# A fused eight-batch transformer kernel: front of the cross stage in halves, shared one-hots, final sums on TensorE

## The reference, cut to what matters

```python
ln1 = _layer_norm(hidden_states, ln1_weight, ln1_bias)      # cross stage begins
qkv = jnp.einsum('sbh,oh->sbo', ln1, qkv_weight)
... # causal attention, projection
h1 = hidden_states + proj
ln2 = _layer_norm(h1, ln2_weight, ln2_bias)
logits = x @ router_weight                                   # x is ln2 by token
top_p, top_i = jax.lax.top_k(probs, K)                       # K = 2
...
dst = jnp.where(valid, sorted_exp * cap + within, T)
padded_tokens = jnp.zeros((T, H), x.dtype).at[dst].set(x[order // K], mode='drop')
fc1 = jax.nn.gelu(jnp.einsum('ech,ehf->ecf', xt, moe_w1))
fc2 = jnp.einsum('ecf,efh->ech', fc1, moe_w2).reshape(T, H)
moe_out = jnp.zeros((N, H)).at[padded_tid].add(fc2 * padded_probs[:, None])
return h1 + moe_out.reshape(S, B, H)     # then x = x + gb * (this), the layer's gate
```

## Time and profile before

| | us |
|---|---|
| median of the runs | 3152.18 |
| the profiled execution, own time | 3159.02 |
| its span | 3157.3 |
| cross stage, from its first to its last instruction | 2499.9 to 2754.5 |
| routing, to the last instruction of the table of slots | 2754.8 to 2802.9 |
| experts, first gather to last copy | 2803.8 to 3108.5 |
| last scatters, final sums, stores | 3108.5 to 3157.3 |

### The profile page before, as it was taken

One profiled execution on the slowest core, in us unless ns is written; L12 is line 12 of the kernel. 1 busy time (PEld: TensorE's weight loads), 2 busy tenths in 40 slices (PEclk: granted clock), 3 DMA queues, 4 the chain that ended last, 5 costly groups with the idle time before them and its releaser, 6 DMA issues. The chain is left out here.

```text
span 3157.3 us, 53117 instructions
## 1 busy us (share of the span) xinstructions
PE 2904.5 (92%) x20820; PEld 1968.8 (62%) x20820; DVE 1646.8 (52%) x5006; ACT 1403.8 (44%) x3081; POOL 836.2 (26%) x831
## 2 busy tenths in 40 slices
PE   6889999878999999999999999999999688899993
PEld 3566666654666757576666666665656444478883
DVE  4667776645555544544444444445554488631114
ACT  3666666632535444444444444534444124132222
POOL 1001111113333332332323222233333311025551
PEclk8999999999999999999999999999999899789997
DMA  4111111004000000000010000000000000112325
GB/s 139 18 19 20 18 20 20 8 3 164 8 4 10 6 16 30 1 1 1 13 33 1 1 1 5 28 14 11 6 6 11 11 1 27 53 41 79 73 83 186
DMA packets 66232, 93.95 MB, mean 30 GB/s; under 512 B 9971, under 2 KB 52982, under 8 KB 64944
## 3 DMA queue, kind: packets, MB, share of 16 engines
q1 hardware_dynamic: 58304, 74.24, 8.0%
q0 software_dynamic: 7680, 16.32, 2.0%
HBM read 59.31 MB, written 27.36 MB: 27 GB/s over the span
## 5 line engine op out<-in xcount | busy, mean ns | idle before, releaser
L1343 PE MATMUL bank<-h2T,w 128*128 128x512 f32 x1024 | 478.9, 606 | 5.3 <-ACT gT L1281 3.7
L1381 PE MATMUL bank<-w,gT 128*128 128x256 f32 x2048 | 465.9, 381 | 0.0
L1381 PEld LDWEIGHTS bank<-w,gT 128*128 128x128 f32 x2048 | 379.3, 190 | 49.7 <-issue 0.5
L1018 POOL TENSOR_TENSOR prob<-prob,rsum 128x512 f32<-128x512 f32 (+1 forms) x256 | 237.7, 949 | 591.0 <-DVE rsum L1165 591.0
L1343 PEld LDWEIGHTS bank<-h2T,w 128*128 128x128 f32 x1024 | 182.2, 190 | 224.0 <-issue 173.7
L1281 ACT ACTIVATE gT<-bank,vec 128x512 f32<-128x512 f32 x256 | 175.1, 687 | 285.6 <-PE bank L1343 284.2
L583 ACT ACTIVATE y<-y,least 128x128 f32<-128x128 f32 (+3 forms) x512 | 252.2, 555 | 52.4 <-DVE least L463 52.3
L463 DVE CUSTOM_DVE_ANT_0 y<-bank,mask 128x128 f32<-128x128 f32 (+3 forms) x512 | 223.9, 486 | 71.9 <-PE bank L680 71.0
L1171 DVE COPY probT<-bank 128x1024 f32<-128x1024 f32 (+1 forms) x128 | 139.3, 1088 | 226.7 <-PE bank L1397 226.7
L1142 DVE CUSTOM_DVE_ANT_0 prob<-bank,mask 128x256 f32<-128x256 f32 (+1 forms) x512 | 164.3, 386 | 168.1 <-PE bank L1333 168.1
L1253 ACT ACTIVATE prob<-prob,least 128x256 f32<-128x256 f32 (+1 forms) x512 | 239.9, 473 | 15.8 <-DVE least L1142 15.5
(11 more groups left out here) (313 smaller groups left out, 5010.7 us busy)
## 6 DMA issues: line engine op xcount, KB each, us to landing
w<-in_W SPq DMA_DIRECT2D x8, 1024.0 KB, 5.9
expert_parts<-zeros SPq DMA_DIRECT2D x8, 1024.0 KB, 16.2
we<-in_we SPq DMA_DIRECT2D x16, 512.0 KB
rows<-modulation SPq DMA_DIRECT2D x40, 128.0 KB, 2.9
x<-in_x SPq DMA_DIRECT2D x8, 512.0 KB, 6.3
prob<-score SPq DMA_DIRECT2D x64, 64.0 KB, 2.4
probT<-score SPq DMA_DIRECT2D x64, 64.0 KB, 2.4
token_rows<-rows_normed SPq DMA_DIRECT2D x4, 1024.0 KB, 4.4
```

Of the source, the lines that this page charges most:

```text
L1018: nc.gpsimd.tensor_tensor(two, two, rsum[:, at:at + 2].unsqueeze(2).to_broadcast([P, 2, width]), ALU.mult).then_inc(s["probs"], 1)
L1343: ins = nc.tensor.matmul(M[m % 2][:, :], w1[:, k, m * P:(m + 1) * P], h2T[:, k, :], start=(k == 0), stop=(k == KD - 1))
L1381: ins = nc.tensor.matmul(M[i][:, (t % 2) * D:(t % 2 + 1) * D], gT[:, m, t * P:(t + 1) * P], w2[:, m, :], start=(m == 0), stop=(m == MF - 1))
```

## The change

It has four parts. **(a)** The front of group 0 goes in two halves of four tiles with semaphores of their own (`front_stats`, `front_rstd`, `front_norm`); the clearing of banks 4 and 5 moves behind it and behind the statistics of group 1; PE runs 6 `idle_products` ahead of it. **(b)** In `token_rows` and `expert_parts` a token's row stands by partition, then tile: four rows of one partition are next to each other, so a final load reads 4 KB at a time where it read 1 KB; the token numbers in `c.value` follow. The stores of `token_rows` and of the result still move 1 KB rows. **(c)** In every piece of the routing table DVE makes `lohot` for columns 0 to 3 and ACT for 4 to 7, and PE waits for both. **(d)** ACT turns each share into a diagonal matrix (8 of 128x128 a batch, in the `lohot` buffers), PE adds both halves up in the banks by 8 matmuls a batch, DVE multiplies by the gate out of the banks and adds to `c.x`. PE runs 12 more idle products behind the last expert matmul. SP loads the first halves, ACT's queue the second; SP stores the even batches, ACT the odd.

The diff, without the list of semaphore names, one repeated line of ACT's `norm`, and most unchanged lines:

```diff
...
@@ -1490,6 +1491,7 @@
 LAST_TILE = NT - 1
+AHEAD = TURNS - 1
@@ -1634,7 +1636,7 @@
     sp.dma_start(c.gains[:, :], d["moe_ln"]).then_inc(s["load"], 16)
-    by_place = c.token_rows.rearrange("(b t p) n -> t p b n", t=NT, p=P)
+    by_place = c.token_rows.rearrange("(b p t) n -> t p b n", t=NT, p=P)
@@ -1645,11 +1647,18 @@
+    def rstd_of_half(h):
+        rows = slice(4 * h, 4 * h + 4)
+        pool.wait_ge(s["front_stats"], h + 1)
+        steps(nc.gpsimd.tensor_scalar(ve[:, rows], mv[:, rows, 1], EPS, None, ALU.add))
+        ins = nc.gpsimd.tensor_tensor(rstd[:, rows], ve[:, rows], half8[:, rows], ALU.pow)
+        ins.then_inc(s["front_rstd"], 1)
+
     def rstd_of(p):
-        pool.wait_ge(s["stats1"], TURNS + p + 1)
+        pool.wait_ge(s["stats1"], AHEAD + p + 1)
         if p > 2:
-            pool.wait_ge(s["norm1"], TURNS + p)
+            pool.wait_ge(s["norm1"], AHEAD + p)
@@ -1673,7 +1682,8 @@
     steps(nc.gpsimd.memset(later[:, :], 0.0))
-    rstd_of(0)
+    for h in range(2):
+        rstd_of_half(h)
@@ -1701,7 +1711,8 @@
     nc.gpsimd.tensor_scalar(c.cols[:, :], c.cols[:, :], AWAY, None, ALU.subtract)
-    nc.gpsimd.iota(c.value[:, :], pattern=[[P, PAIRS]], base=1, channel_multiplier=1,
+    nc.gpsimd.iota(c.value[:, :].rearrange("p (i t) -> p i t", t=NT), pattern=[[T, TOPK * B], [1, NT]], base=1,
+                   channel_multiplier=NT,
@@ -1717,16 +1728,15 @@
         steps(ins)
-        if p:
-            dve.wait_ge(s["rstd1"], TURNS + p)
+        if p > 1:
+            dve.wait_ge(s["rstd1"], AHEAD + p)
     def norm(p):
-        dve.wait_ge(s["rstd1"], TURNS + p + 1)
-        if p:
-            full(dve, ("T", (KD - 1, 1), p - 1))
+        dve.wait_ge(s["rstd1"], AHEAD + p + 1)
+        full(dve, ("T", (KD - 1, 1), p - 1))
@@ -1830,10 +1840,21 @@
+    for h in range(2):
+        for i in range(4 * h, 4 * h + 4):
+            ins = nc.vector.bn_stats(bn[:, i, :], c.y[:, i, 0, :])
+        steps(ins)
+        for i in range(4 * h, 4 * h + 4):
+            ins = nc.vector.bn_aggr(mv[:, i, :], bn[:, i, :])
+        ins.then_inc(s["front_stats"], 1)
+    for h in range(2):
+        dve.wait_ge(s["front_rstd"], h + 1)
+        for i in range(4 * h, 4 * h + 4):
+            ins = nc.vector.tensor_scalar(xn[:, i, :], c.y[:, i, 0, :], mv[:, i, 0:1], rstd[:, i:i + 1],
+                                          ALU.subtract, ALU.mult)
+        ins.then_inc(s["front_norm"], 1)
+    stats(1)
     nc.vector.memset(c.bank[:, 4:6, :], 0.0).then_inc(s["aux"], 1)
-    stats(0)
-    norm(0)
-    stats(1)
@@ -1941,8 +1962,10 @@
                 k, g = i
-                if k == 0 and g == 0:
-                    pe.wait_ge(s["norm1"], TURNS + p + 1)
+                if k == 0 and p == 0:
+                    pe.wait_ge(s["front_norm"], g + 1)
+                if k == 0 and g == 0 and p:
+                    pe.wait_ge(s["norm1"], AHEAD + p + 1)
@@ -2022,6 +2045,7 @@
+    idle_products(c, 6, 0)
@@ -2055,6 +2079,7 @@
 PIECE = 8
+HALF = PIECE // 2
@@ -2111,7 +2136,14 @@
 def tokens(dram, b):
-    return dram[b * T:(b + 1) * T, :].rearrange("(t p) n -> p t n", p=P)
+    return dram[b * T:(b + 1) * T, :].rearrange("(p t) n -> p t n", p=P)
+
+def sums(b):
+    at = 2 * (b % 3)
+    return c.bank[:, at:at + 2, :].rearrange("p i (t n) -> p (i t) n", n=D)
+
+def diagonal(b, i, t):
+    return lohot[b % 2][:, i * NT + t, :]
@@ -2135,8 +2167,7 @@
         sp.dma_start(c.y[:, b], tokens(c.parts[0:B * T, :], b)).then_inc(s[f"landed{min(b, B - 2)}"], 16)
-        sp.dma_start(rows(b), tokens(c.parts[B * T:2 * B * T, :], b)).then_inc(s[f"landed{min(b, B - 2)}"], 16)
-    for b in range(B):
+    for b in range(0, B, 2):
@@ -2228,10 +2259,9 @@
             dve.wait_ge(s["pairs_used"], x - 1)
-        if x % 2 == 0:
-            nc.vector.tensor_tensor(lohot[0][:, :, :], c.lows[:, :, :].to_broadcast([P, PIECE, P]),
-                                    low[:, PIECE * x:PIECE * (x + 1)].unsqueeze(2).to_broadcast([P, PIECE, P]),
-                                    ALU.is_equal)
+        at = PIECE * x
+        nc.vector.tensor_tensor(lohot[x % 2][:, 0:HALF, :], c.lows[:, :, :].to_broadcast([P, HALF, P]),
+                                low[:, at:at + HALF].unsqueeze(2).to_broadcast([P, HALF, P]), ALU.is_equal)
@@ -2268,24 +2298,19 @@
-    def summed(b):
-        dve.wait_ge(s["scaled"], b + 1)
-        for t in range(NT):
-            k = b * NT + t
-            ins = nc.vector.scalar_tensor_tensor(out=c.y[:, b, t, :], in0=rows(b)[:, t, :],
-                                                 scalar=share[:, 1, k:k + 1], in1=c.y[:, b, t, :],
-                                                 op0=ALU.mult, op1=ALU.add)
-        ins.then_inc(s["summed"], 1)
+    def gated(b):
+        dve.wait_ge(s["summed"], b + 1)
+        nc.vector.tensor_tensor(c.y[:, b], sums(b), row_of(gate, b).to_broadcast([P, NT, D]), ALU.mult)\
+          .then_inc(s["sums_read"], 1)
     def finished(b):
-        dve.wait_ge(s["summed"], b + 1)
-        steps(nc.vector.tensor_tensor(c.y[:, b], c.y[:, b], row_of(gate, b).to_broadcast([P, NT, D]), ALU.mult))
+        dve.wait_ge(s["sums_read"], b + 1)
         if b < B:
-            summed(b)
+            gated(b)
@@ -2295,17 +2320,17 @@
     act.wait_ge(s["lows_ready"], 1)
-    for x in range(1, PAIRS // PIECE, 2):
+    for x in range(PAIRS // PIECE):
             act.wait_ge(s["pairs_used"], x - 1)
-        for m in range(PIECE):
+        for m in range(HALF, PIECE):
             k = PIECE * x + m
-            ins = nc.scalar.activation(lohot[1][:, m, :], c.lows[:, 0, :], ACT.Abs, bias=minus_low[:, k:k + 1],
-                                       scale=1.0)
+            ins = nc.scalar.activation(lohot[x % 2][:, m, :], c.lows[:, 0, :], ACT.Abs,
+                                       bias=minus_low[:, k:k + 1], scale=1.0)
         ins.then_inc(s["low_away"], 1)
-        act.wait_ge(s["low_away"], x // 2 + 1)
-        nc.scalar.activation(lohot[1][:, :, :], lohot[1][:, :, :], ACT.Relu, bias=c.ones[:, 0:1], scale=-1.0)\
-          .then_inc(s["low_hots"], 1)
+        act.wait_ge(s["low_away"], x + 1)
+        hots = lohot[x % 2][:, HALF:PIECE, :]
+        nc.scalar.activation(hots, hots, ACT.Relu, bias=c.ones[:, 0:1], scale=-1.0).then_inc(s["low_hots"], 1)
@@ -2323,13 +2348,30 @@
             gain(j + 1)
+    def stored(b):
+        act.wait_ge(s["finished"], b + 1)
+        nc.scalar.dma_start(out[b].rearrange("(t p) n -> p t n", p=P), c.x[:, b]).then_inc(s["stored"], 16)
+
     for b in range(B):
-        act.wait_ge(s[f"landed{min(b, B - 2)}"], 32 if b < B - 2 else 64)
-        for t in range(NT):
-            k = b * NT + t
-            ins = nc.scalar.activation(c.y[:, b, t, :], c.y[:, b, t, :], ACT.Identity, bias=c.zero[:, :],
-                                       scale=share[:, 0, k:k + 1])
+        if b == 2:
+            for z in range(BUFS):
+                act.wait_ge(s[("scattered0", "scattered1", "scattered2", "scattered3")[z]],
+                            16 * TT * (ALL_CHUNKS // BUFS))
+            for at in range(B):
+                nc.scalar.dma_start(rows(at), tokens(c.parts[B * T:2 * B * T, :], at))\
+                  .then_inc(s[f"landed{min(at, B - 2)}"], 16)
+        if b >= 4 and b % 2 == 0:
+            stored(b - 3)
+        if b >= 2:
+            act.wait_ge(s["summed"], b - 1)
+        for i in range(TOPK):
+            for t in range(NT):
+                k = b * NT + t
+                ins = nc.scalar.activation(diagonal(b, i, t), c.ident[:, :], ACT.Identity, bias=c.zero[:, :],
+                                           scale=share[:, i, k:k + 1])
         ins.then_inc(s["scaled"], 1)
+    for b in (B - 3, B - 1):
+        stored(b)
@@ -2342,8 +2384,7 @@
         pe.wait_ge(s["hots_ready"], x + 1)
-        if x % 2:
-            pe.wait_ge(s["low_hots"], x // 2 + 1)
+        pe.wait_ge(s["low_hots"], x + 1)
@@ -2396,6 +2437,20 @@
     down(ALL_CHUNKS - 1)
+    pe.wait_ge(s["down_out"], ALL_CHUNKS)
+    for _ in range(12):
+        nc.tensor.matmul(c.bank[:, 7, :], c.ident[:, :], w2[1][:, 0:2, :].rearrange("p k n -> p (k n)"), start=True,
+                         stop=True)
+    for b in range(B):
+        pe.wait_ge(s["scaled"], b + 1)
+        pe.wait_ge(s[f"landed{min(b, B - 2)}"], 32 if b < B - 2 else 64)
+        if b >= 3:
+            pe.wait_ge(s["sums_read"], b - 2)
+        for t in range(NT):
+            for i, x in enumerate((c.y[:, b], rows(b))):
+                ins = nc.tensor.matmul(sums(b)[:, t, :], diagonal(b, i, t), x[:, t, :], start=(i == 0),
+                                       stop=(i == TOPK - 1))
+        ins.then_inc(s["summed"], 1)
```

(15 more changed lines are left out.)

15 lines of the change are left out of this document (removed), and 3 rows, old and new, of the table SEMS.

## The result

The changed kernel took 3148.89 us (median of 20 runs, 3143.95 to 3155.27), the kernel before 3152.93 beside it (20 runs, 3150.62 to 3157.69): a ratio of 0.9984, 95% interval 0.9977 to 0.999. By that interval it is 3.2 to 7.3 us less, a small gain; the medians differ by 4.0, less than the 0.2% (6.3 us) that the prediction set as its bound. The forecast was 3150.4.

The account below looks back on a forecast made before the run. Three chained stretches were taken to bound it: the front's DVE-POOL-PE chain, half-clock PE in the table, and PE in the new sums. -2.9 - 1.5 + 2.6 = -1.8 from 3152.18 gave 3150.4 us, range 3142 to 3157.5.

Parts of the forecast that it names:

- Front: Front of the cross stage: projections start at 2510.5 instead of 2513.4, -2.9 us (bounds -4.2 and -1.9).
- Rival D: Front: idle products end after 2509.4, so nothing is won there; total 3153.3 us, chance 0.10.
- Row order: Final loads: 4 KB rows land faster, 21.3 instead of 24.0 us, but hide behind PE and are worth nothing.
- more than 1 us each: Final sums: sign that the forecast is wrong, ACT held by its own DMA issues for more than 1 us each.
- Table: Routing table: three pieces at full clock, then five at half clock, -1.5 us (bounds +0.5 and -7.4).
- as much pausing in all. So I take the fall: Routing table: PE pauses as much as before in all, so its clock falls as before; -1.5 us.
- rival B: Routing table: the clock stays full throughout, -7.4 us there instead of -1.5; total 3144.5 us, chance 0.18.
- Sums: Final sums: PE bounds them at 3.45 a batch, with two pauses of 2.1 and one clock loss; +2.6 us.
- Rival A: Final sums: a batch costs PE about 0.9, so loads bind; -9.3 there, total 3138.5 us, chance 0.06.
- Rival C: Final sums: a stall drops PE's clock for good, a batch takes 6.9; +7.9, total 3160.1 us, chance 0.06.
- the bound of two losses: Final sums: both pauses, not one, are followed by a slow batch, each loss +1.96 us; part of the +6.5 bound.
- The offset: Whole kernel: the profiled execution lies 6.8 us above the median, taken as unchanged by the change.

Follow-up runs that it names:

- Experiment 1: The kernel before with only the front in halves and its 6 idle products: ratio 0.9986, 3152.17 us.
- experiment 5: The kernel before with only the new row order, loads still all on SP: ratio 1.0001, 3154.89 us.
- experiment 6: The changed kernel with the old row order, final loads in 1 KB rows: ratio 1.0007, 3157.09 us.
- experiments 1, 5 and 8: The kernel before with the front alone, the row order alone, and the final sums with the new layout alone: ratios 0.9986, 1.0001 and 1.0015.
- experiment 7: The changed kernel with the old row order and all final loads issued by SyncE: ratio 0.9982, 3150.26 us.
- experiment 3: The kernel before with only the new routing table, its one-hots shared by DVE and ACT: ratio 0.9981, 3149.25 us.
- experiment 2: The changed kernel without the 6 idle products ahead of the front: ratio 0.9968, 3145.05 us.

## Why the prediction was right

The forecast, 3150.4, was 1.5 above the median of 3148.89. That closeness is in part luck. As a difference the forecast was -1.8, where the medians differ by 4.0: the direction was right and the size less than half. The time came closer than the difference because the base, the median of three runs, lay 0.75 below the 3152.93 that twenty runs gave. And the difference itself was no further off because errors of opposite sign stood in it. By its own steps, in the profile pair:

- **Front, predicted -2.9, measured -2.1 to the first projection and -1.0 behind it.** The mechanism held: the idle products set the start, and the transposes behind them ran at full clock. I took 7.5 for the products between bounds of 6.9 and 8.4; they took 8.44, just beyond the upper bound, and this 0.9 is the whole shortfall. That the full clock would also shorten the first scores (3.50 to 2.14) was not in the sum. Experiment 1 gives 1.3 to 7.9 for the front alone. Rival D did not happen, but it was close: counted from the start of the cross stage, which lies 2.3 earlier in this profile, the products ended at 8.5 and the transposes of before began at 9.5 (its 2509.4).

- **Row order, predicted to be worth nothing.** Alone that holds but for the 0.7 up to the first landing (experiment 5). Beside part (d) it fails: without it the sums would have been 6.7 longer (experiment 6). The step that failed is that I priced the loads by their landing alone, and ScalarE's issue by SP's first (0.37). The rest of SyncE's queue behind that row, which I did not look at, already had it: in the trace of before SP needs 1.41 to 2.33 for each load from the seventh on. In rows of 4 KB the issues are short (the longest of ScalarE's eight took 0.97 in the changed kernel, so the sign "more than 1 us each" did not come), so the forecast for the kernel as changed was not hurt.

- **Table, predicted -1.5, measured -7.7.** This step was wrong. DVE's pace of 2.5 a piece was right (2.45), PE's 1.9 to 2.0 too, and the upper bound of -7.4 is what came. What failed is "as much pausing in all. So I take the fall": there was less pausing than the sum had, 0.44 beside 2.01 of work (18% of the time) and not 0.6 beside 1.9 (24%; before, 1.8 of 7.7, 23%), and in these evenly spaced pieces the clock stayed full in eight profiles of nine, where the order of the earlier trace rows, with its pause of 1.32, was followed by a fall sooner or later in all four profiles that have it (before, and experiments 1, 5 and 8: 46.5, 46.5, 45.7 and 42.9). I had one table to read and took its outcome for a property of the matmuls. Since the fall still comes now and then (experiment 7), the mean gain lies below the 7.7 of the pair; experiment 3 has 3.2 to 8.8. What in the new order keeps the clock, the even spacing, the shorter single pause or the smaller share of pauses, was not tried by itself. So in the table rival B is what happened, and in the profile pair its total nearly came too: -7.4 by the stages, where B has -7.7. Its 3144.5 did not come as a median. That the table's gain is smaller on the mean is one part of that; the rest was not traced, since the other executions have no profile.

- **Sums, predicted +2.6, measured +4.4.** The mechanism was right in every part: PE and no load on the chain, two pauses ahead of batches 4 and 6, released by the diagonals behind ScalarE's store, one slow batch (5.40; 5.41 was taken from the earlier trace rows). Two terms were too small. Each pause was 2.1 in the sum and 2.69 and 2.66 in the trace, since eight diagonals take 3.19 and not 2.45. They read their scale from memory, the instruction of the earlier trace rows has it fixed. The Trainium skill ("ScalarE: Activation LUTs", section "What ACT_TABLE_LOAD costs") gives about 93 ns for each operand that is a pointer to a column; as an estimate from that, eight more of them cost 8 x 0.093 = 0.74, and 3.19 - 2.45 is 0.74 too. And the batches cost 27.92 in one piece, 0.3 more than 8 x 3.45.

- **Rival A** fell with the 3.49 a batch, four times the 0.87 that its rule gives. The Trainium skill has a reason on another page ("FP8 and Floating Point Precision", section "TensorE Precision Notes"): true float32 takes four passes. **Rival C** did not come; the clock returned within the slow batch in the profile of after (7.19 for the two batches after the second pause). In the profile of experiment 2 those two took 8.87, so the second loss comes now and then, and the bound of two losses was well taken.

- **The sum.** By the stages -7.4, by the medians -4.0, by the ratio -3.2 to -7.3. The three parts alone give -4.4, -6.0 and +4.7 from their ratios, together -5.7. Against the -1.8 of the forecast the table is short by 4.5 and the front by 1.5, and the sums give 2.1 of it back. The experts' stretch, which the change leaves alone, differs by -1.0 in the pair and lies between 303.9 and 306.5 over all profiles; I take that for scatter.

- **The offset.** I put all stages on the profile of before, a long execution, and took off the 6.8 by which it lay above the median, which is the same as adding -1.8 to the median. The profile of after lies only 0.4 above its own median; that is why the two profiles differ by 9.7 and the medians by 4.0.

## What to carry to other kernels

Before a wait or a DMA is put on a compute engine's queue, list what stands behind it in program order, and put first what another engine is waiting for: two lines moved were worth 7.4 us of the last stretch here, and 5.7 by the ratios, where the medians give the whole change 4.0. Price a DMA's issue on such a queue by the last of a row of issues, and not by the first. Where the granted clock of one stretch carries most of an edit's worth, one profile of it is one draw: look at the same stretch in several before its outcome is taken as a rule.

## What the runs showed of the hardware

- A queue that issues loads of 0.524 MB in rows of 1 KB is held for 1.42 us each from about the seventh on when all are on one queue, and ScalarE's for 2.5 to 2.9 each from its fifth on when it and SyncE issue eight each; in rows of 4 KB SyncE's eight of sixteen took 4.37 in all (experiments 6 and 7, and the changed kernel).
- Rows of 4 KB landed at 400 to 419 GB/s in three 4 us windows of two kernels each, rows of 1 KB at 348 to 361. The Trainium skill ("DMA: Bandwidth & Descriptors", section "Where 436 GB/s comes from") lets about 358 GB/s on the HBM side bind such transfers; with this kernel's one core running, the former went beyond it.
- In the new table PE's matmuls of 80 columns kept the full clock (granted 1.00 over 20 us) at 2.0 us of work and 0.44 us of pause by turns in eight of nine profiles.
- An ACTIVATE of 128x128 took 0.31 us with one pointer operand (2.45 for eight) and 0.40 with two (3.19 for eight).
